# One gated cross-attention and ternary feed-forward layer: the negated key maximum, the tile sums and the order of five engines

## The reference, cut to what matters

```python
emb = layernorm(x) + ctx
q, k, v = emb@wq+bq, emb@wk+bk, emb@wv+bv
ek = exp(k - max over tokens of k)
ew = exp(w - max_w)          # w = pos_bias where |i-j| < 64, else 0: constant far away
y  = sigmoid(q) * (ew @ (ek*v)) / (ew @ ek)
a  = layer_norm(y@wo + bo + emb) * gamma + beta
ff = relu(a@w1 + b1) @ w2 + b2          # 256 -> 1024 -> 256
x  = x + tanh(g0) * layer_norm(ff + a)
# second block: activations rounded to 8 bits per token, weights to -1, 0, 1
x  = x + tanh(g1) * down(round(silu(gate(xq)) * up(xq)))   # 256 -> 1024 -> 256
```

## Time and profile before

| what | us |
|---|---|
| median of 3 runs (lowest 508.49, highest 514.18) | 509.64 |
| the profiled execution's own time | 508.42 |
| its span, first to last instruction | 506.7 |
| PE busy | 477.5 |
| DVE, ACT, POOL busy | 428.9, 385.0, 247.2 |
| mean granted TensorE clock | 0.974 of full |

### The profile page before, as it was taken

One profiled execution on the slowest core, in us unless ns is written; L12 is line 12 of the kernel. 1 busy time (PEld: TensorE's weight loads), 2 busy tenths in 40 slices (PEclk: granted clock), 3 DMA queues, 4 the chain that ended last, 5 costly groups with the idle time before them and its releaser, 6 DMA issues.

```text
span 506.7 us, 10223 instructions
## 1 busy us (share of the span) xinstructions
PE 477.5 (94%) x3096; PEld 394.2 (78%) x3096; DVE 428.9 (85%) x1067; ACT 385.0 (76%) x711; POOL 247.2 (49%) x389
## 2 busy tenths in 40 slices
PE   8689989999999999999999999989999999999695
PEld 8478777888887788868887889768887887898253
DVE  7698886969898788988988969997889898967985
ACT  2564589679689949897679955997468967978884
POOL 8553073127832309632762466541673751288611
PEclk9978799999999999999999999999999999999899
DMA  6763104212301133322231243112213310430001
GB/s 220 217 208 126 64 22 100 67 21 56 94 21 31 33 43 116 73 43 43 75 92 23 61 96 95 22 22 63 74 53 63 105 23 1 63 105 2 0 22 63
DMA packets 64004, 34.48 MB, mean 68 GB/s; under 512 B 41936, under 2 KB 63440, under 8 KB 63952
## 3 DMA queue, kind: packets, MB, share of 16 engines
q1 hardware_dynamic: 62848, 33.83, 25.8%
q10 hardware_dynamic: 1104, 0.00, 0.1%
HBM read 20.20 MB, written 4.19 MB: 48 GB/s over the span
## 4 chain that ended last, share of the span: by engine, by line
PE 67%; DVE 6%; issue 5%; ACT 4%; POOL 3%; DVEq 0%; ACTq 0%; POOLq 0%
PE ps L2551 40%; PE ps L2717 8%; PE ps L2619 7%; PE ps L2739 4%; PE ps L2570 2%; PE ps L2602 2%; PE ps L2634 2%; DVE cols L1788 1%; DVE work L1782 1%; PE ps L2559 1%; PE ps L2573 1%; PE ps L2652 1%; ACT et L911 1%; DVE work L1634 1%; POOL rstd L560 1%
## 5 line engine op out<-in xcount | busy, mean ns | idle before, releaser
L2551 PE MATMUL ps<-w_hi,h_hi 128*128 128x256 f32 x256 | 75.9, 297 | 0.0
L2551 PE MATMUL ps<-w_lo,h_hi 128*128 128x256 f32 x256 | 71.4, 279 | 0.0
L2551 PE MATMUL ps<-w_hi,h_lo 128*128 128x256 f32 x256 | 71.3, 279 | 0.0
L557 POOL TENSOR_TENSOR mv<-mv,cols 128x2 f32<-128x2 f32 x64 | 12.5, 195 | 115.4 <-DVE mv L1653 115.1
L946 ACT ACTIVATE h_hi<-ps,cols 128x512 fp32r<-128x512 f32 (+1 forms) x72 | 46.9, 653 | 26.4 <-PE ps L2551 19.0
L1743 DVE TENSOR_TENSOR h_lo<-ps,h_hi 128x512 fp32r<-128x512 f32 (+1 forms) x72 | 44.3, 623 | 15.8 <-ACT ps L951 14.9
L1708 DVE RECIPROCAL ps<-ps 128x512 f32<-128x512 f32 x16 | 53.8, 3361 | 4.0 <-PE ps L2634 4.0
L2551 PE MATMUL ps<-n1T_hi,w_hi 128*128 128x512 f32 (+1 forms) x144 | 55.2, 383 | 1.7 <-DVE n1T_lo L1737 1.7
L2551 PE MATMUL ps<-n1T_hi,w_lo 128*128 128x512 f32 (+1 forms) x144 | 53.0, 368 | 0.0
L2551 PE MATMUL ps<-n1T_lo,w_hi 128*128 128x512 f32 (+1 forms) x144 | 52.9, 367 | 0.0
L2551 PEld LDWEIGHTS ps<-w_hi,h_hi 128*128 128x128 f32 x256 | 48.2, 188 | 3.8 <-issue 1.1
(11 more groups left out here) (193 smaller groups left out, 1502.4 us busy)
## 6 DMA issues: line engine op xcount, KB each, us to landing
x_in<-in_x_dram SPq DMA_DIRECT2D x16, 256.0 KB, 3.1
emb<-in_ctx_dram SPq DMA_DIRECT2D x16, 256.0 KB, 3.0
work<-in_x_dram SPq DMA_DIRECT2D x8, 512.0 KB, 4.3
out_dram<-work SPq DMA_DIRECT2D x16, 256.0 KB, 2.2
work<-in_L_xattn_w_dram SPq DMA_DIRECT2D x2, 1024.0 KB, 7.2
work<-in_L_ffn_w_gate_dram SPq DMA_DIRECT2D x1, 1024.0 KB, 7.9
place_c<-in_L_ffn_w_down_dram SPq DMA_DIRECT2D x1, 1024.0 KB, 4.8
work<-in_L_ffn_w_up_dram SPq DMA_DIRECT2D x1, 1024.0 KB, 5.2
```

Source lines behind the costliest of these rows:

```text
L2551: last = nc.tensor.matmul(dst, lhsT, rhs, start=(i == 0 and not begun), stop=(i == n - 1 and ends))
```

## The change

Four edits of instructions, and new lists.

1. The maximum is taken negated by the reduction itself, and per head one step of two operations, (-max - bk) + bk with bk as column operand twice, replaces the add and the subtract on both heads. Each exponential waits for its own head's step.
2. The tile sums are copied to `stage` unrounded, three times over, by ACT. After the transpose ACT rounds them into `esum_hi`, and a new DVE step, `sum_lower`, reads `esum_hi` and the PSUM bank to make the rows of `esum` that need it the remainder. `attend_far` waits for that. `lo_sums` is one more small reduction in `far_masks`.
3. `beta_w1` is cut from four pieces to eight.
4. `BANK` and the lists of all five engines are new.

```diff
-                nc.vector.tensor_reduce(mx[:, h:h + 1], bank(b, "kT", h), AX.X, ALU.max).then_inc(kmax_ok.sem, 1)
+                nc.vector.tensor_reduce(nmax[:, h:h + 1], bank(b, "kT", h), AX.X, ALU.max, negate=True).then_inc(kmax_ok.sem, 1)
...
-            def neg_max(b):
-                wait(dve, kmax_ok, b, 2)
+            def neg_max(b, h):
+                wait(dve, kmax_ok, b, h + 1)
                 dve.wait_ge(load["vectors1"], 16 * VECTORS1)
-                nc.vector.tensor_tensor(mxb, mx, bk_col, ALU.add).then_inc(mxb_ok.sem, 1)
-                wait(dve, mxb_ok, b, 1)
-                wait(dve, ek_ok, b, 0)
-                nc.vector.tensor_tensor(nmx, bk_col, mxb, ALU.subtract).then_inc(nmx_ok.sem, 1)
+                wait(dve, ek_ok, b, h - 1)
+                nc.vector.tensor_scalar(nmx[:, h:h + 1], nmax[:, h:h + 1], bk_col[:, h:h + 1], bk_col[:, h:h + 1],
+                                        ALU.subtract, ALU.add).then_inc(nmx_ok.sem, 1)
...
-            def tile_sums(b):      # on DVE
-                wait(dve, ek_ok, b, ND * NT)
-                wait(dve, ekv_ok, b, ND * NT)
-                wait(dve, s_ps, b, 0)
-                dve.wait_ge(far_rows_ok, 1)
-                nc.vector.tensor_copy(stage[:, :, 0:16].rearrange("p g (a n) -> p g a n", n=8)[:, :, :, 0:NT],
-                                      tsum[:, :, None, :].to_broadcast([P, 4, 2, NT])).then_inc(sums_hi_ok.sem, 1)
-                wait(dve, sums_hi_ok, b, 1)
-                nc.vector.tensor_tensor(stage[:, :, NT:2 * NT], tsum[:], stage[:, :, 0:NT], ALU.subtract).then_inc(sums_lo_ok.sem, 1)
+            def sum_lower(b):      # on DVE
+                wait(dve, s_hi_ok, b, 1)
+                dve.wait_ge(far_rows_ok, 5)
+                wait(dve, den_ps, b, 0)
+                wait(dve, num_ps, b, 0)
+                nc.vector.scalar_tensor_tensor(esum[:], esum_hi[:].bitcast(F32), lo_sums, bank(b, "S")[:, 0:P], ALU.mult, ALU.add).then_inc(s_lo_ok.sem, 1)
...
+            def tile_sums(b):      # on ACT
+                wait(act, ek_ok, b, ND * NT)
+                wait(act, ekv_ok, b, ND * NT)
+                wait(act, s_ps, b, 0)
+                act.wait_ge(far_rows_ok, 1)
+                nc.scalar.activation(stage[:, :, 0:3 * NT].rearrange("p g (a n) -> p g a n", n=NT),
+                                     tsum[:, :, None, :].to_broadcast([P, 4, 3, NT]), ACT.Copy).then_inc(sums_ok.sem, 1)
...
+                nc.vector.tensor_reduce(lo_sums, groups[:, :, NT:2 * NT], AX.XY, ALU.add, negate=True).then_inc(far_rows_ok, 1)
```

More of the change, by code:

```diff
@@ L1849, in _ @@
             wkv_lower()
-            ewT_lower(0)
+            position_max(1)
             key_max(0, 0)
+            wq_lower()
             key_max(0, 1)
-            neg_max(0)
+            neg_max(0, 0)
+            neg_max(0, 1)
+            wo_lower()
             weighted(0, 0, 0)
+            far_weights()
+            ewT_lower(1)
+            ewT_lower(2)
+            ewT_lower(3)
             weighted(0, 0, 1)
@@ L1860, in _ @@
             weighted(0, 3, 0)
-            position_max(1)
+            weighted(0, 3, 1)
             e_lower(0, 0)
+            tile_stats(1, 0, 0)
+            tile_stats(1, 0, 1)
+            mean_variance(1, 0, 0)
             e_lower(0, 1)
             e_lower(0, 2)
-            weighted(0, 3, 1)
-            wq_lower()
-            wo_lower()
-            far_weights()
-            tile_stats(1, 0, 0)
-            tile_stats(1, 0, 1)
+            e_lower(0, 3)
+            sum_lower(0)
             tile_stats(1, 0, 2)
-            mean_variance(1, 0, 0)
@@ L1919, in _ @@
-            e_lower(1, 1)
-            weighted(1, 3, 0)
-            e_lower(1, 2)
-            weighted(1, 3, 1)
-            tile_sums(1)
-            bit_clip(0)
+            e_lower(1, 2)
+            e_lower(1, 3)
+            bit_clip(0)
+            n1_lower(0, 0)
+            b1_whole()
+            sum_lower(1)
             n1_lower(0, 1)
+            gated(1, 0)
             bit_scale(1)
-            e_lower(1, 3)
-            bit_clip(1)
-            gated(1, 0)
+            inverse(1, 0)
@@ L2138, in _ @@
             weighted(4, 3, 1)
-            tile_sums(4)
-            product(1, 3)
-            product_scale(1, 3)
+            mean_variance(2, 2, 1)
             e_lower(4, 0)
@@ L2394, in _ @@
+            divided(7, 0)
+            tile_stats(5, 3, 2)
+            hidden_lower(6, 3)
+            y_lower(7, 0)
+            gated(7, 1)
+            tile_stats(5, 3, 3)
+            mean_variance(5, 3, 1)
+            inverse(7, 1)
+            hidden_lower(6, 4)
+            divided(7, 1)
+            hidden_lower(6, 5)
+            y_lower(7, 1)
+            product(5, 0)
             token_max(5, 1)
             token_scales(5, 1)
-            hidden_lower(6, 3)
-            inverse(7, 0)
@@ L3224, in _ @@
             attend(7, "den", 0, 2)
+            attend(7, "num", 0, 0)
+            attend(7, "den", 1, 1)
+            attend(7, "den", 1, 2)
+            down(4, 2)
+            attend(7, "den", 1, 3)
             attend(7, "den", 0, 3)
-            attend_far(7, "den", 0)
-            attend_far(7, "den", 1)
+            sums_T(7)
             attend(7, "num", 0, 1)
             attend(7, "num", 0, 2)
+            feed_forward(6, 0)
+            attend_far(7, "den", 0)
+            hidden(6, 2)
+            feed_forward(6, 1)
+            down(4, 3)
+            hidden(6, 3)
             attend(7, "num", 0, 3)
             attend_far(7, "num", 0)
+            feed_forward(6, 2)
+            attend(7, "num", 1, 0)
+            attend(7, "num", 1, 1)
+            attend(7, "num", 1, 2)
+            attend(7, "num", 1, 3)
             attend_far(7, "num", 1)
+            gate(5, 0)
+            attend_far(7, "den", 1)
+            up(5, 0)
+            hidden(6, 4)
             hidden(6, 5)
```

1982 lines of the change are left out of this document (982 added, 1000 removed), and 15 rows, old and new, of the table BANK.

## The result

The changed kernel takes 496.15 us (median of 4 runs, 495.52 to 496.99), the one before 510.23 beside it (4 runs, 508.49 to 514.18); the ratio is 0.9715 [0.9656, 0.9774], so 2.85% faster. The forecast was 503 in a range of 497 to 511: right in sign, too small by half, and 0.85 us outside the range. The profiled executions took 508.42 and 496.12 us, spans 506.7 and 494.4, so the traces have 12.3 us of it to explain, where my sum had 6.8. The rest of the gap between the medians is on the side of the kernel before: its 17 runs of one batch have spans of 506.5 to 507.5 us in four of them and 510.7 to 514.6 in thirteen, the latter at a mean clock of 0.965 to 0.971 in place of 0.974 to 0.978, while the changed kernel's eight runs of two batches stay between 492.6 and 495.2 us, and why is open.

A forecast was written before the change was run, and what follows sets the result against it. PE was taken as the bound, busy 477.5 of 506.7 us. Terms -1.5 + 0.3 - 5.5 + 1.5 - 1.6 = -6.8 took 508.4 to 501.6; adding 1.2 gave 502.8, forecast 503, range 497 to 511.

The forecast's parts named there:

- The maximum: Negated maximum with one-column steps: the stretched subtract goes, 2.1 us off the first exponential, counted in the start; other batches nothing.
- The tile sums: Sums staged on ACT, split by sum_lower: DVE 4.4 us less busy, PE's 1.5 us wait goes, -1.5.
- The start: Before 84 us: queries, far row and transposes ahead of e_rows(0) save idle and half clock; -5.5, ends -2 and -8.
- landmark of `y_lower`: Start of y_lower(0,1), expected near 49.5 us against 54.91 before; the start's -5.5 was set near it.
- idle term: Within the start: PE's two idles at e_rows(0) and the first attend, 3.9 us, plus 0.6 left of L2619's total.
- clock term: Within the start: about 2.3 us saved from some 4.6 us of PE work done at half clock.
- Start-up: One more small reduction in far_masks and positions fetched ahead of the context: between 0 and 0.6 us, taken +0.3.
- The middle: From 84 to 468 us: less PE work covers the chain between project and n1_rows; +1.5, ends -3 and +6.
- sums wait: PE's 1.5 us wait for the second tile-sums step, expected to go: -1.5.
- second rival: Slower: the norm chain behind project becomes PE's wait in the eight batches; 508.5 or 516.5 us; chance 0.13.
- The end: After 468 us: five gate and up steps move ahead, two batch 6 products leave DVE's tail; -1.6, ends -4 and +4.8.
- The first rival: Head start not kept: PE ahead at 40 us waits at the first hidden steps; start -2, time 506.3; chance 0.31.

The follow-up runs named there:

- two-step kernel: The changed kernel with each head's bias made by a dependent subtract and add on a column instead of one two-operation step; 499.34 us, ratio 0.9732.
- second profile: The changed kernel profiled again with nothing changed; lost time 26.6 us at 84 us and 53.1 at the end, against 28.5 and 54.9 in its first profile.
- query cover alone: Changed instructions in the old order, batch 0's query products and their needs ahead of e_rows(0,0), w2's low parts moved later on GpSimd; 509.24 us, ratio 0.9945.
- old-start kernel: The changed kernel with every engine's list and the DMA order as before up to about 92 us; 505.94 us, ratio 0.9899.
- the kernel that waited from 38 to 45 us: Changed instructions in the old order, query products ahead of e_rows(0,0), w2's low part left heading GpSimd's list; 521.87 us, ratio 1.0187.

## Why the prediction was wrong

The mechanism was right in kind: less idle time of PE at both ends. Three terms of the sum were too small, the start's above all. By step:

- **The maximum.** Right. The stretch (2.1 us forecast off the first exponential) is shown by the two-step kernel (2.6 us). ACT began only 0.7 us earlier, since the second maximum in front of it came later: it started at 22.68 against 20.96, with PE at half clock from 18.5 us on and wq's split ahead of it on DVE. In the second profile, at full clock, ACT began 1.7 us earlier.
- **The tile sums.** Rows right to 5%. "Worth on PE's path: the 1.5 us wait of the earlier trace rows goes, -1.5" did not hold in the old order, where 1.6 us of waits for `sum_lower` took its place. In the new order neither wait is left, and the old sums put back there cost 4.9 us.
- **The start** is the step that failed: "I take -5.5, near the landmark of `y_lower`", between ends of -2 and -8. It measured -8.0, at the far end, and -9.9, beyond it, in the second profile. I counted 3.9 + 0.6 us of idle. The 3.9 lay before 31 us, and 3.8 of it went in the first profile, 2.1 in the second. The 0.6 I read as batch 0's, but it stands at 69 us, in batch 1. The stretch to 84 us of the earlier trace rows had 12.5 us of idle, and I never said where the rest lay: 4.0 us between 36 and 84 us, in waits of 1.7, 0.7, 0.6, 0.6 and 0.3 us (n1T_lo, embT_hi, e_lo, ew_lo, ev), of which I had only that 0.6. The new order of that stretch removes them all, and putting the old order back there costs 3.1 to 4.9 us of span. In sum the idle before 84 us fell by 7.0 us (12.5 to 5.5; by 5.8 in the second profile) where I had 4.5. The clock gave 1.6 us where I had 2.3, but 5.1 in the second profile (an estimate: half of 17.0 less 13.8 or 6.8 us). So the idle term was too small, and the clock term is a matter of which profile one takes. The landmark misled too: `y_lower(0,1)` starts at 53.59 against 54.91, hardly earlier, since work of batch 1 had been pulled in front of it. The cause was half wrong: the query cover alone gave nothing at the end.
- **Start-up.** +0.3 forecast; the first `keys_T` starts 0.14 us later than before in the first profile and 0.15 us earlier in the second. Nothing.
- **The middle.** With the sums wait, 0 forecast, -1.4 measured. The second rival's wait did not appear: PE idles 1.4 us from 84 to 440. The longest wait of PE there is 1.0 us, for a DMA.
- **The end.** -1.6 forecast, -2.9 measured, between -4 and +4.8. The five steps moved ahead cost the 5 us forecast (4.8). What they free is 8.0 us, from `second_residual(7,1)` to the end (41.5 to 33.5), where I had 6.4.
- **The first rival**, a head start lost again at the first hidden steps, did not come: PE idles 0.2 us from 36 to 84 us. With the old order of that stretch a part of it does come, 1.1 us for n1's low part. And what is ahead at 84 us is still ahead at 440, by the old-start kernel.

The terms: 8.0 + 1.4 + 2.9 = 12.3, against 5.2 + 0 + 1.6 = 6.8. All three missed on the same side, since each had been set between a gain read from rows and a doubt, and no doubt came true. The middle's +1.5 had no row behind it.

**Open:** what brings the clock to half at 43 us and why it stays there 10.3 us in one profile and 6.8 in another, and what makes it longer again when the query products go ahead.

## What to carry to other kernels

Before pricing a new order, put every microsecond of the bounding engine's idle time down to a wait with a place, to the end of the stretch, and price each; the part left without a name was about 3 of the 5.5 us missed here, by the second profile. When a step moves ahead, the heads of all other queues that feed it or feed on what it displaced move with it, GpSimd's too: one forgotten split cost 13 us. With PE 96% busy the head start reached the end here, and a step on another engine was worth something else than the wait it had shown in the old order: putting the old sums back cost 4.9 us, the wait had been 1.5.

## What the runs showed of the hardware

- A VectorE tensor_tensor with both inputs in SBUF waits for a GpSimd addition even with one element per partition: 1.90 us against 0.158. A tensor_scalar with the same operands, issued inside such an addition in four kernels, took 0.259 to 0.267 us, as it does elsewhere.
- A tensor_scalar of 128x2048 and GpSimd additions of 128x1024 take turns. It took 1.23 us alone; issued inside an addition it ended 1.1 us after that addition did, and took 2.35 or 3.41 us by how much of it was left. The addition issued into it took 3.10 in place of 2.40 us.
- TensorE fell to half clock near 43 us in the changed kernel, for 10.3 us in one profile and 6.8 in the other, with PE busy in every microsecond ahead of it from 36 us, and did so whether or not its one-column matmuls stood together. In the kernel that waited from 38 to 45 us, half clock lasted from 40 to 67 us.
